# Adding the shared expert's output to a stored copy of x by accumulating transfers

## What is computed

```python
x = x + out_routed(x) + gemma_mlp(x, shared_gate, shared_up, shared_down)
x = x + x @ W_base.T + b_base + lora(x, w) * 2
# gemma_mlp: (gelu(x @ gate) * (x @ up)) @ down, with 1024 inner features
# out_routed: the same with each sequence's 2 best of 8 experts, weighted
```

## Time and profile before

| | |
|---|---|
| Median of 3 runs | 797.29 us (796.95 to 797.66) |
| Profiled execution, its own time | 796.85 us |
| Its span in the trace | 795.0 us |
| Between the two, outside the span | 1.85 us |
| PE busy, share of the span | 789.5 us, 99% |
| DVE busy | 668.8 us, 84% |
| ACT busy | 478.5 us, 60% |
| POOL busy | 278.4 us, 35% |
| 16 DMA engines, mean share | 43.7% |

### The profile page before, as it was taken

The page is one execution under the profiler, slowest core; times in us unless marked ns, Lnnn a source line. Parts: engine busy times, 40 slices in busy tenths (PEclk is TensorE's granted clock), DMA queues, the critical chain, the costliest instruction groups (busy, mean ns, idle before and its releaser), DMA issues.

```text
span 795.0 us, 13413 instructions
## 1 busy us (share of the span) xinstructions
PE 789.5 (99%) x4133; PEld 681.1 (86%) x4133; DVE 668.8 (84%) x910; ACT 478.5 (60%) x737; POOL 278.4 (35%) x284
## 2 busy tenths in 40 slices
PE   8999999999999999999999999999999999999998
PEld 7888888888888888888888889888898888898887
DVE  4866888888887899889888898888898889889886
ACT  6554564564664666656666666666666666566653
POOL 1621321321430363263352444425435234532520
PEclk9999999999999999999999999999999999999999
DMA  7436506304726632563563275346336426631400
GB/s 204 123 80 200 144 1 198 121 1 146 233 72 206 222 116 80 171 184 101 165 189 95 90 224 153 105 141 189 106 125 215 124 80 198 172 108 51 133 2 27
DMA packets 138894, 105.21 MB, mean 132 GB/s; under 512 B 62928, under 2 KB 131280, under 8 KB 138832
## 3 DMA queue, kind: packets, MB, share of 16 engines
q1 hardware_dynamic: 138832, 104.53, 43.7%
HBM read 79.86 MB, written 24.64 MB: 131 GB/s over the span
## 4 chain that ended last, share of the span: by engine, by line
PE 99%; DMA 0%; DVE 0%; ACT 0%; SPq 0%; DVEq 0%; issue 0%
PE ps_ring L827 61%; PE ps_acc L827 36%; DMA raw<-_L_cond_shared_gate_dram 0%; PE ps_acc L1039 0%; PE ps_ring L848 0%; PE ps_ring L853 0%; PE ps_ring L857 0%; PE ps_acc L1059 0%; DVE stage L1925 0%; PE ps_acc L944 0%; PE ps_ring L1059 0%; ACT xc L1165 0%; PE ps_acc L1085 0%; ACT wide L1165 0%; SPq L517 0%
## 5 line engine op out<-in xcount | busy, mean ns | idle before, releaser
L827 PE MATMUL ps_ring<-xc,wide 128*128 128x512 f32 (+1 forms) x1926 | 416.2, 364 | 0.0
L827 PEld LDWEIGHTS ps_ring<-xc,wide 128*128 128x128 f32 x1926 | 336.8, 189 | 59.4 <-DVE post L1568 0.6
L1165 ACT CAST inner_hi<-post 128x512 fp32r<-128x512 f32 x192 | 117.7, 621 | 102.9 <-DVE post L1857 31.8
L827 PE MATMUL ps_acc<-inner_hi,wide 128*128 128x512 f32 x504 | 171.0, 390 | 0.0
L1511 DVE TENSOR_TENSOR inner_lo<-post,inner_hi 128x512 fp32r<-128x512 f32 x192 | 146.3, 769 | 9.0 <-ACT inner_hi L1165 6.1
L1168 ACT ACTIVATE post<-ps_ring 128x512 f32<-128x512 f32 (+1 forms) x125 | 68.0, 546 | 103.4 <-PE ps_ring L827 98.0
L827 PEld LDWEIGHTS ps_acc<-inner_hi,wide 128*128 128x128 f32 x504 | 94.8, 188 | 19.1
L827 PE MATMUL ps_acc<-inner_lo,wide 128*128 128x512 f32 x252 | 98.4, 391 | 0.0
L1168 ACT ACTIVATE post<-post 128x256 f32<-128x256 f32 (+1 forms) x98 | 53.7, 563 | 53.4 <-DVE post L1798 36.3
L827 PE MATMUL ps_acc<-inner_hi,sh_dn 128*128 128x512 f32 x256 | 83.9, 389 | 0.0
L1857 DVE SCALAR_TENSOR_TENSOR post<-post,coef_now,ps_ring 128x512 f32<-128x512 f32 x66 | 49.3, 747 | 36.2 <-PE ps_ring L827 34.1
(11 more groups left out here) (126 smaller groups left out, 1015.5 us busy)
## 6 DMA issues: line engine op xcount, KB each, us to landing
rights_scratch<-xc SPq DMA_DIRECT2D x6, 1792.0 KB, 10.2
raw<-n_L_cond_skill_gate_dram SPq DMA_DIRECT2D x32, 256.0 KB, 3.0
raw<-in_L_cond_skill_up_dram SPq DMA_DIRECT2D x32, 256.0 KB, 3.5
raw<-n_L_cond_skill_down_dram SPq DMA_DIRECT2D x32, 256.0 KB, 3.9
xbuf<-n_L_cond_skill_gate_dram SPq DMA_DIRECT2D x32, 256.0 KB, 3.0
xbuf<-in_L_cond_skill_up_dram SPq DMA_DIRECT2D x32, 256.0 KB, 3.5
xbuf<-n_L_cond_skill_down_dram SPq DMA_DIRECT2D x32, 256.0 KB, 3.8
xt_scratch<-xbuf SPq DMA_DIRECT2D x8, 512.0 KB, 3.3
```

The source lines that it names most:

```text
L827: last = pe.matmul(dst, left_[a], right_[b], start=start and n == 0, stop=stop and n == len(PASSES) - 1, skip_group_check=adds)
L1165: return nc.scalar.copy(dst, src)
```

## The change

`sh_dram` and POOL's `row_sum` are gone. SP's `store_xt` now stores the transposed x of each sequence twice, to `xt_dram` and to a new DRAM tensor `base_dram` (`base_scratch`). The two halves of `stage` are no longer stored by SP; a new function `add_shared`, in POOL's queue, adds them to `base_dram` with an accumulating transfer each. A row then loads `base` already with x in it, and DVE waits for that load itself. The first row's load of `xf` for POOL is gone, the other rows' load of `xf` no longer waits for `base_ready`.

```diff
-        sh_dram = nc.dram_tensor("sh_scratch", [B, P, HC * S], F32, kind="Internal").ap()
+        base_dram = nc.dram_tensor("base_scratch", [B, P, HC * S], F32, kind="Internal").ap()
...
-                sp.dma_start(xt_dram[2 * qn + r], xbuf[:, r * 2 * S:(r + 1) * 2 * S]).then_inc(xt_stored[r], 16)
...
-            def store_shared(q):
-                sp.wait_ge(acc0_out, 2 * (q + 1))
-                to, what = shared_place(q, 0)
-                sp.dma_start(to, what).then_inc(sh_stored, 16)
-                sp.wait_ge(acc1_out, 2 * (q + 1))
-                to, what = shared_place(q, 1)
-                sp.dma_start(to, what).then_inc(sh_stored, 16)
+
+                for to in (xt_dram, base_dram):
+                    sp.dma_start(to[2 * qn + r], xbuf[:, r * 2 * S:(r + 1) * 2 * S]).then_inc(xt_stored[r], 16)
...
-                if q > 0:
-                    store_shared(q - 1)
...
-                sp.wait_ge(xt_stored[r], 16 * Q)
+                sp.wait_ge(xt_stored[r], 32 * Q)
...
-            store_shared(Q - 2)
...
-                    sp.dma_start(base, sh_dram[b]).then_inc(base_landed, 16)
+                    sp.dma_start(base, base_dram[b]).then_inc(base_landed, 16)
...
-                    sp.dma_start(xf, xt_dram[b]).then_inc(xf_landed, 16)
...
-                    store_shared(Q - 1)
...
-                    sp.wait_ge(base_ready, b + 1)
...
+            def add_shared(q):
+
+                for r in range(2):
+                    pool.wait_ge(xt_stored[r], 32 * (q + 1))
+                pool.wait_ge(acc0_out, 2 * (q + 1))
+                to, what = shared_place(q, 0)
+                pool.dma_start(to, what, accum_op=ALU.add).then_inc(sh_stored, 16)
+                pool.wait_ge(acc1_out, 2 * (q + 1))
+                to, what = shared_place(q, 1)
+                pool.dma_start(to, what, accum_op=ALU.add).then_inc(sh_stored, 16)
...
+                if q > 0 and j == 0:
+                    add_shared(q - 1)
...
-            def row_sum(b):
-
-                pool.wait_ge(base_landed, b * 16 + 16)
-                for n in range(4):
-                    part = slice(n * HS, (n + 1) * HS)
-                    done = G.tensor_tensor(base[:, part], base[:, part], xf[:, part], ALU.add)
-                done.then_inc(base_ready, 1)
...
+                    add_shared(Q - 1)
...
-                dve.wait_ge(xt_stored[r], 16 * qn)
+                dve.wait_ge(xt_stored[r], 32 * qn)
...
-                dve.wait_ge(base_ready, b + 1)
+                dve.wait_ge(base_landed, b * 16 + 16)
```

More of the change, by code:

```diff
@@ L373, in cond_resid_kernel @@
         c22_done = sem("c22_done")
-        base_ready = sem("base_ready")
         x_rows = x.rearrange("b (p t) h -> b p t h", t=TT)
@@ L677, in _, with shared_place @@
                             base=0, pattern=[[-1, P]], channel_multiplier=1).then_inc(ident_ready, 1)
+            def shared_place(q, n):
+                if q == 0:
+                    return base_dram[n], stage[:, n, :]
+                return (base_dram[2 * q:2 * q + 2].rearrange("r p (m h t) -> p m h r t", m=HC, h=2)[:, :, n],
+                        stage[:, n, :].rearrange("p (m r t) -> p m r t", m=HC, r=2))
+            def add_shared(q):
[7 more added lines that the diff above has]
+                pool.dma_start(to, what, accum_op=ALU.add).then_inc(sh_stored, 16)
             def left_sums(j):
@@ L786, in ex_c22 @@
                 last.then_inc(ex_c22_done, 1)
-            def row_sum(b):
-                pool.wait_ge(base_landed, b * 16 + 16)
-                for n in range(4):
-                    part = slice(n * HS, (n + 1) * HS)
-                    done = G.tensor_tensor(base[:, part], base[:, part], xf[:, part], ALU.add)
-                done.then_inc(base_ready, 1)
             def row(b, first, last):
                 if first:
+                    add_shared(Q - 1)
                     pool.wait_ge(sh_stored, 16 * B)
                     sums_of_weights(b, 1)
-                    row_sum(b)
                     ex_c22(b, 1)
@@ L1487, in row @@
                     if k == X_STEP and not last:
-                        act.wait_ge(xf_landed, b * 16 + 32)
+                        act.wait_ge(xf_landed, b * 16 + 16)
                         if first:
@@ L1905, in _ @@
             row(B - 1, 1, False, True)
-            dve.wait_ge(base_ready, B)
+            dve.wait_ge(base_landed, B * 16)
             for c in range(HC):
```

## The result

| | before | changed |
|---|---|---|
| Median | 797.35 us (796.95 to 797.66, 4 runs) | 804.35 us (802.27 to 804.76, 4 runs) |
| Ratio, 95% interval | | 1.0083 [1.0065, 1.0101] |
| Profiled execution, its span | 796.85, 795.0 us | 802.27, 800.4 us |

The change makes the kernel 0.8% slower; I had forecast no change. In a second group of runs the same kernel gave 803.72 us against 796.87, 1.0091 [1.0076, 1.0105]; one run of the kernel before took 981.51 us there, at a mean granted clock of 0.754, and is left out.

The account below looks back on a forecast made before the run. TensorE, running products back to back, was taken as the bound, so relief elsewhere wins nothing. Four terms of 0 us on the earlier kernel's median of 797.29 gave 797.3 us, range 796.0 to 800.3.

Parts of the forecast that it names:

- the additions land late: Rival, chance 0.12: accumulating transfers landing beyond 9.2 us stall unit 13 first, then the first row; 802.9 us at 11.2.
- What bounds the kernel: Whole kernel: TensorE runs product behind product from about 7 us; relieving POOL, DVE or queues wins at most 0.6 us.
- I take 6 us, near the serial sum: Landing time assumed for the additions of stage, near a store plus a load one behind the other, 6.9 us.
- L: Time from the second half of stage being full until sh_stored tells POOL it has landed; taken as 6 us.
- the two stalls that were to be 0 us: TensorE's stalls in unit 13 and the first row, each forecast as 0 us with landing after 6 us.
- 11.2 us as a far end: Slowest transfer of this size in the earlier trace, the upper bound for the landing; it would cost 5.6 us.
- The formula of the first row: First row: slack through POOL, ACT and DVE is 4.4 us, so TensorE stalls by L - 8.9; forecast 0 us.
- The formula of unit 13: Unit 13: slack behind POOL's sums and c22 is 3.83 us, so TensorE stalls by L - 7.9; forecast 0 us.
- Units 5 and 9 at 0 us: Units 5 and 9: t_a starts 0.85 us later but is wanted only by the next pair's work; 0 us.
- The start: Extra stores delay unit 3's weights by at most 3.9 us against 4.1 slack: 0 us; rival of 799.2, chance 0.03.
- DVE holds up POOL's transfers: Rival, chance 0.03: DVE locks POOL out while it writes descriptors, two holds for each issue; 803.1 us.

## Why the prediction was wrong

It said 797.3 us, in a range of 796.0 to 800.3, with 0.76 on no change. The median is 804.35 us, beyond the range and beyond the 802.9 us of the rival "the additions land late", which is the one that came about and had 0.12.

**What bounds the kernel: right.** TensorE without slack, nothing to win by relieving others. The kernel without `row_sum` shows it: 41.6 us of additions away from POOL, 797.00 against 797.01 us.

**The step that failed: "I take 6 us, near the serial sum".** L was 8.3 us in unit 13 and 12.4 in the first row, and the two stalls that were to be 0 us were 0.7 and 3.1 (weight load). Three things were missing in it.
- I priced one transfer, but `sh_stored` counts two. They are issued 0.95 us apart and share the same 16 engines. A single addition is near what I took: in the kernel with a semaphore for each half POOL's sums of unit 13 start 6.0 us after the first issue (204.76 to 210.72). Two are 7.2 us of all engines, whatever the latency of one.
- The store and the load of the earlier trace rows are landing times. What I needed was the engines' time, and the profile had a way to it for transfers that it did show: the share of a queue times the span over its bytes, 43.7% of 795.0 us for the 104.5 MB of SP's queue before, or 3.3 us per MB. That is 1.7 us of the 3.5 to a store's landing. With it the question would have been how much more an addition costs, and twice 3.3 us per MB would have been a fair guess for reading and writing; measured are 6.5.
- In the first row the additions meet 1.8 MB of loads. I wrote this down as a point for the rival and left it out of the sum. With these loads held back L was 8.6 us there, 3.8 less.

I even had 11.2 us as a far end from the trace, and treated it as a rare outlier. In the first row of the changed kernel the second addition took 11.6 us from its issue to its landing.

**The formula of the first row: right.** L - 8.9 gives 3.5 us, measured 3.1. In all seven profiles where TensorE stalls for these sums (for 0.6 to 3.7 us) it lies 0.4 us too high, and 0.3 of that is that POOL's four sums now take 2.9 us instead of 3.3. So this slack, read from the timeline link by link, was sound.

**The formula of unit 13: near the number, by another path.** L - 7.9 gives 0.4 us, and TensorE's seventh product starts 0.5 us late (222.61, after 18 matmuls from 218.05 that need until 222.14). But `c22` wasn't what it waited for. L grew by 4.3 us; the four sums then took 2.9 us instead of 4.8, since POOL wasn't held up as it was at L715 in the earlier trace rows, and `c22` ended at 218.46. Its reader would have started at 218.55 (217.40 before, and `stage` is full 1.15 us later here). DVE came to that reader only at 220.14, because its own instructions had run beside POOL's late ones, 1.17 and 1.78 us instead of 0.68 and 0.69. The changed kernel:

```profile
216.14 1.17 DVE L1587 TENSOR_TENSOR post<-post 128x512 f32<-128x512 f32 x1
217.23 1.78 DVE L1503 TENSOR_TENSOR inner_lo<-post,inner_hi 128x512 fp32r<-128x512 f32 x1
...
220.14 0.68 DVE L1587 TENSOR_TENSOR post<-post 128x512 f32<-128x512 f32 x1
...
216.72 1.74 POOL L706 TENSOR_TENSOR post<-post 128x512 f32<-128x512 f32 x1
```

and before:

```profile
215.00 0.68 DVE L1595 TENSOR_TENSOR post<-post 128x512 f32<-128x512 f32 x1
215.60 0.69 DVE L1511 TENSOR_TENSOR inner_lo<-post,inner_hi 128x512 fp32r<-128x512 f32 x1
```

In the kernel with a semaphore for each half, where POOL is earlier, these two take 0.72 and 0.68 us again and the wait is gone. So it is the same cost as in units 5 and 9 below. That the formula came so close is luck. It doesn't have the wait of 0.67 us in the next unit at all; it is gone too when the first half has its own semaphore, but its path I haven't followed. A better L would have given 797.3 + 3.5 + 0.4 = 801.2 us, still 3.1 us under the median.

**Units 5 and 9 at 0 us: wrong by 1.1 us together** (0.82 + 0.86 instead of 0.31 twice). I had followed `t_a` to its reader and found it far away. But `t_a` had run in a gap of POOL, and now stands ahead of `c22`, `t_b` and `t_c`, which all move 0.6 us against DVE's sums. In the changed kernel, POOL and DVE after the landing:

```profile
92.46 1.30 POOL L737 TENSOR_TENSOR stage<-xbuf 128x512 f32<-128x512 f32 x1 [5.29 <-DMA base_scratch<-stage]
93.72 1.29 POOL L706 TENSOR_TENSOR post<-post 128x512 f32<-128x512 f32 x1
94.97 1.28 POOL L749 TENSOR_TENSOR stage<-xbuf 128x512 f32<-128x512 f32 x1
...
95.03 1.78 DVE L1587 TENSOR_TENSOR post<-post 128x512 f32<-128x512 f32 x1
```

DVE's addition of two SBUF operands took 1.27 us in the kernel before and takes 1.78 here, and 0.68 us when POOL rests. TensorE waited for the end of this chain already, so 0.5 us of DVE is 0.5 us of time. The Trainium skill, "SBUF — State Buffer", SBUF: two separate sides, has a port pair that these two engines share, and an addition of two SBUF operands on DVE contends for it with a POOL instruction that reads SBUF; the trace agrees, with 1.78 us against 0.68. The kernel with a semaphore for each half brings `t_a` of unit 5 back to 90.27 and both waits to 0.31 us.

**The start: right.** Two stores for one, 797.03 us. In the changed kernel ACT's cast of unit 3's weights started at 42.07 instead of 41.18, and TensorE was not late.

**DVE holds up POOL's transfers: didn't happen.** The issues grew to 1.45 and 1.98 us, but in the kernel with plain transfers, with DVE as busy, they are 0.92 us each in the same places. What makes them longer is the accumulation. The 0.03 on this rival had its effect (a long L) for another reason.

**The clock** was in none of my terms. In three of six traces some 1.7 us followed from the stall.

## What to carry to other kernels

For a transfer that someone waits for, count the work of the DMA engines, not only the landing time: all transfers behind the same semaphore, and all that other queues move meanwhile. An accumulating transfer moves its data in place of an engine's addition, but here it took 6.5 us of all 16 engines per MB where others took 3.2; put it where nobody wants its source buffer for some 8 us, or 12 in a crowded stretch, or give each half a semaphore and send the wanted half first, which won back 6 of the 7 us here. And when a step moves later, look at what it pushes back on its own engine and what that now runs beside on another, not only at who reads it.

## What was unexpected of the hardware

- Accumulation of 512 KB from SBUF to DRAM in pieces of 1 KB: 3.6 us of all 16 engines. All eight have three times the packets of plain ones (3456 against 1152) and more than twice the engines' share (3.4% against 1.4%); at equal packets, in unit 5, it is still 6.1 against 2.6 us for the pair.
- POOL's time to issue one rises with it, from 0.92 us to 1.45 and 1.98; with the rows of 4 KB of unit 5 it was 1.02 and 1.18, where plain ones took 0.69 and 0.55.
- A plain store of `stage` landed after 4.0 us in the median from POOL's queue, and 3.5 from SP's. The prediction quoted a difference of 0.4 us to the first byte between the two queues from the Trainium skill, "DMA: Bandwidth & Descriptors", Specifications. The traces have the landing and not the first byte; with 0.5 us they are in line.
- Around or behind stalls of TensorE of 3.3 to 3.7 us the granted clock was 0.66 to 0.93 in one or two windows of 5 to 10 us in three executions, some 1.7 us lost each time; behind 2.8, 3.1 and 3.3 us it stayed at 1.00 in three others.
- Still open: what makes the last landing differ by half a microsecond between executions of the same kernel (11.4 to 12.0 us from the second issue to POOL's first sum in four traces) and the waits for `v57` by 1 us, which stalls the clock forgives, and how the 7 us of the median split between waits and clock.
